# Loading a low-rank factor from SyncE's queue, behind x's first half, instead of from ScalarE's

## What is computed

```python
def qlora_linear(x, q, scale, bias, la, lb):       # la: 32 x 256, lb: 256 x 32
    w = (q / 7.5 - 1) * repeat(scale, 16)          # q: integer codes 0 to 15
    return x @ w.T + bias + (x @ la.T) @ lb.T
# branch 1: xn + linear attention(xn) (16 heads of 16, elu + 1), then a layer norm with gamma and beta
# branch 2: three blocks h = qlora(gelu(layernorm(qlora(h)))) + h, with h = xn at the start
out = x + branch1(xn) + branch2(xn)
```

## Time and profile before

| | us |
|---|---|
| median of 3 runs | 616.52 |
| lowest and highest | 616.03, 617.02 |
| the profiled execution, its whole time | 616.88 |
| its span | 615.2 |
| TensorE busy in the span | 590.7 |
| VectorE busy | 526.9 |
| ScalarE busy | 402.8 |
| GpSimd busy | 373.9 |

### The profile page before, as it was taken

How to read it: one execution, slowest core, us unless ns; L and a number is a source line. 1 busy time by engine, 2 the same in 40 slices (tenths; PEclk the granted TensorE clock), 3 DMA queues, 4 the chain that set the end, 5 groups by cost and what they waited for, 6 DMA issues and landing times.

```text
span 615.2 us, 10218 instructions
## 1 busy us (share of the span) xinstructions
PE 590.7 (96%) x3285; PEld 498.3 (81%) x3285; DVE 526.9 (86%) x1164; ACT 402.8 (65%) x619; POOL 373.9 (61%) x361
## 2 busy tenths in 40 slices
PE   6999999999999999999999999999999999999986
PEld 5778879778897889868797788978889688987865
DVE  3679899798888989889897988979898898989797
ACT  2776656848667577766768576684876667775552
POOL 5745766557644766457665575556754576746574
PEclk9999999999999999999999999999999999999999
DMA  9103000500032000500004000230004000030001
GB/s 241 62 2 136 1 2 35 170 2 0 1 125 80 0 0 18 180 6 0 0 35 170 0 0 0 87 118 0 0 0 173 32 0 0 34 102 1 0 2 69
DMA packets 11461, 29.00 MB, mean 47 GB/s; under 512 B 2593, under 2 KB 4273, under 8 KB 11441
## 3 DMA queue, kind: packets, MB, share of 16 engines
q1 hardware_dynamic: 10960, 28.35, 13.7%
q10 hardware_dynamic: 480, 0.41, 0.3%
HBM read 20.37 MB, written 8.39 MB: 47 GB/s over the span
## 4 chain that ended last, share of the span: by engine, by line
PE 70%; ACT 9%; POOL 7%; DVE 6%; issue 6%; DMA 1%; ACTq 1%; DVEq 0%; POOLq 0%
PE bank L1478 19%; PE bank L1484 9%; PE bank L1594 7%; PE bank L1605 7%; PE bank L1649 6%; PE bank L1551 4%; PE bank L1616 4%; PE bank L1570 3%; ACT fw L630 3%; POOL gl L262 2%; ACT L630 2%; PE bank L1578 2%; PE bank L1561 2%; PE bank L1538 2%; PE bank L1471 2%
## 5 line engine op out<-in xcount | busy, mean ns | idle before, releaser
L262 POOL TENSOR_TENSOR gl<-fw,gh 128x512 fp32r<-128x512 f32 x80 | 104.2, 1319 | 49.4 <-DVE gh L937 37.5
L417 POOL TENSOR_TENSOR sqs<-fw 128x512 f32<-128x512 f32 x48 | 62.8, 1309 | 73.8 <-ACT fw L620 73.7
L620 ACT ACTIVATE fw<-bank,b1c 128x512 f32<-128x512 f32 x96 | 62.3, 686 | 57.8 <-PE bank L1484 57.8
L630 ACT ACTIVATE fw<-fw,vec 128x512 f32<-128x512 f32 x96 | 74.6, 808 | 14.2 <-DVE fw L923 13.9
L923 DVE SCALAR_TENSOR_TENSOR fw<-bank,b1c,rb 128x512 f32<-128x512 f32 x96 | 67.7, 745 | 16.1 <-ACT rb L626 15.8
L267 POOL TENSOR_TENSOR hTl<-hT,hTh 128x512 fp32r<-128x512 f32 x40 | 54.1, 1368 | 39.8 <-ACT hTh L639 33.0
L392 POOL TENSOR_TENSOR rsf<-vef,neghalf 128x4 f32<-128x4 f32 x48 | 50.6, 1055 | 43.7 <-DVE vef L914 43.0
L1605 PE MATMUL bank<-K,XN 128*128 128x256 f32 x256 | 61.7, 382 | 0.0
L1649 PE MATMUL bank<-M,qT 128*128 128x256 f32 x256 | 59.4, 379 | 0.0
L392 POOL TENSOR_TENSOR rs<-ve,neghalf 128x2 f32<-128x2 f32 (+1 forms) x48 | 41.9, 874 | 22.8 <-DVE ve L1020 17.1
L1605 PEld LDWEIGHTS bank<-K,XN 128*128 128x128 f32 x256 | 46.5, 190 | 7.6 <-DVE K L982 2.0
(11 more groups left out here) (157 smaller groups left out, 1593.0 us busy)
## 6 DMA issues: line engine op xcount, KB each, us to landing
X<-in_L_attn_x_dram SPq DMA_DIRECT2D x16, 512.0 KB, 6.7
RES<-in_L_attn_x_dram SPq DMA_DIRECT2D x16, 512.0 KB, 4.3
out_dram<-RES SPq DMA_DIRECT2D x14, 512.0 KB, 2.7
XNB<-in_L_ffn_qweights_dram SPq DMA_DIRECT2D x2, 512.0 KB, 6.6
out_dram<-RES SPq DMA_DIRECT2D x4, 256.0 KB, 2.1
RES<-in_L_ffn_qweights_dram SPq DMA_DIRECT2D x1, 512.0 KB, 8.8
Y<-in_L_ffn_lora_a_dram ACTq DMA_DIRECT2D x4, 96.0 KB, 6.6
Wp<-in_L_attn_Wq_dram SPq DMA_DIRECT2D x1, 256.0 KB, 7.6
```

The costliest lines, as they stand in the source:

```text
L262: engine.tensor_tensor(gl[:, h, m, :], fw[:, h, m, :], gh[:, h, m, :].bitcast(F32), ALU.subtract).then_inc(g_low[h][m], 1)
L417: pool.tensor_tensor(sqs[:, h, :], fw[:, h, 0, :], fw[:, h, 1, :], ALU.add).then_inc(sqs_ready[h], 1)
L620: act.activation(fw[:, h, m, :], FB[h][m][:], ACT.Square, bias=b1c[:, m, j:j + 1]).then_inc(sq_ready[h], 1)
L630: act.activation(fw[:, h, m, :], fw[:, h, m, :], ACT.Gelu, bias=lnb[:, m, j:j + 1], scale=lng[:, m, j:j + 1]).then_inc(g_ready[h], 1)
```

## The change

The four transfers of A are issued by SyncE directly after x's first half and ahead of lb. They carry the same bytes to the same place and raise the same semaphore. ScalarE issues its seven short vectors as before and then goes on.

```diff
@@ -274,6 +274,12 @@
+            def load_lora():
+                for l in range(2):
+                    for c in range(NC):
+                        sp.dma_start(la[(2 * l + c) * R:(2 * l + c + 1) * R],
+                                      lora_a.rearrange("(j two) r d -> two r j d", two=2)[l]).then_inc(w_la, 16)
+
@@ -319,6 +325,7 @@
             def head():
                 load_x(0, 0)
+                load_lora()
                 load_small()
                 load_codes(0)
@@ -574,12 +581,6 @@
-            def load_lora():
-                for l in range(2):
-                    for c in range(NC):
-                        act.dma_start(la[(2 * l + c) * R:(2 * l + c + 1) * R],
-                                      lora_a.rearrange("(j two) r d -> two r j d", two=2)[l]).then_inc(w_la, 16)
-
@@ -692,7 +693,6 @@
             def head():
                 load_vectors()
-                load_lora()
                 ln1_normalise(0, 0, None)
```

## The result

The changed kernel takes 619.47 us (median of 5 runs, 618.57 to 619.63) against 616.58 us for the kernel before (5 runs, 616.03 to 617.02): a ratio of 1.0038, 95% interval 1.0027 to 1.0049. It is slower, by 2.9 us between the medians. The profiled execution took 619.47 us with a span of 617.7, against 616.88 and 615.2.

A forecast was written before the change was run, and what follows sets the result against it. TensorE, busy 96% of the span, was taken as the bound. A gain of 1.95 us less 1.51 of transfer and 0.68 of pace gave +0.24 us: 616.8 us, range 615.4 to 618.3.

The forecast's parts named there:

- rival 2: lb lands at 8.35, filler behind it slow throughout, L1745 at 15.0: 1.9 us slower, 618.4 us; chance 0.18.
- Weight 0 was hidden: GpSimd scales weight 0 near 11.0 us, before TensorE's L1739 is ready for it at 12.7: no cost.
- The step from L1676 to L1745: On TensorE, from the bias vectors' transposes to the product of A: 0.95 us.
- A's way: Transfer of A's 0.393 MB ahead of lb at 260 GB/s: 1.51 us, so lb lands at 7.35 instead of 5.84.
- 7.67 for lb by its issue alone: lb's landing if issued at 3.07 instead of 1.24 with its 4.6 us way unchanged; set aside for the queue's bytes.
- the filler's pace: The 24 filler rows behind lb run partly slow after the pause: 0.68 us lost, L1676 at 12.4.
- Both times for the step: Step to TensorE's fast pace: at 10.2 us if work before the pause counts, at 12.3 if not.
- the upper bound, all slow: All 24 filler rows behind lb at the slow pace: 4.92 us, L1676 at 13.1.
- Hidden, by 0.1: VectorE's weight 0 mean, behind six masked copies, ends at 15.8, before ScalarE's L688 can begin at 15.93: no cost.
- K: Start of L1676, the bias vectors' transposes on TensorE: 10.21 us before, forecast at 12.4.
- 1.95: Most that removing TensorE's wait for A could gain in us: L1745 at 11.16 instead of 13.11.

The follow-up runs named there:

- run 2: Changed kernel with all four filler groups ahead of lb's transposes, so TensorE has no pause: 616.31 us, ratio 0.9998 to the kernel before.
- run 6: Changed kernel without the three filler groups behind lb's transposes, the first group kept: 618.36 us, ratio 1.0026 to the kernel before.
- run 1: Changed kernel with A still on SyncE but directly behind lb (x, lb, A, scales, codes 0): 618.16 us, ratio 1.0018 to the kernel before.
- run 10: Changed kernel with A moved behind codes 0 in SyncE's queue (x, lb, scales, codes 0, A): 616.24 us, ratio 0.9984 to the kernel before.
- run 8: Changed kernel with SyncE's loads reordered (A behind codes 0, several others moved) and all filler ahead of lb's transposes: 615.46 us, ratio 0.9974 to the kernel before.
- run 5: Kernel before, with all four filler groups ahead of lb's transposes and A still on ScalarE's queue: 616.89 us, ratio 1.0010.
- run 12: Changed kernel measured again without any edit, 12 runs: 618.73 us, ratio 1.0029 to the kernel before.
- run 3: Kernel before, with lb alone moved behind scales and codes 0, A staying on ScalarE's queue: 620.07 us, ratio 1.0063.
- run 7: Changed kernel with one filler group more ahead of lb's transposes, nothing taken from behind: 617.84 us, ratio 1.0021 to the kernel before.
- run 9: Changed kernel with the load order of run 8, but the filler where it was in the kernel before: 616.02 us, ratio 0.9984 to that kernel.
- run 4: Changed kernel with lb's transposes written to an idle bank of their own: 618.56 us, ratio 1.0036 to the kernel before.
- run 11: Changed kernel with A behind lb and scales, ahead of codes 0: 617.59 us, ratio 1.0007 to the kernel before.

## Why the prediction was wrong

The forecast was no change, +0.24 us; the measured 619.47 lies above the range, whose end was 618.3. What happened is rival 2, which had 0.18. In the first profile its L1745, put at 15.0, came at 14.92: lb was 2.2 us later and not 2.5, and nearly all of the filler was slow, as given. What this profile lost beyond those 1.9 us is the wait for the bank, which no part of the prediction has.

**Right.** The wait for A vanished and the wait for lb took its place. Codes 0, Wq, Wk and the codes of weights 2 and 3 stayed hidden: L1739 had no wait for GpSimd in the changed kernel, at weight 0 or at weight 2. Weight 0 was hidden by less than it seemed: it was scaled at 11.69, not near 11.0, since its codes landed at 9.7 and not at 9.1. The step from L1676 to L1745 was put at 0.95 and is 0.99. Runs 2 and 6 show that the cover of codes 0 is the filler itself: with L1676 at 10.3 or 9.0, weight 0 waits 1.5 to 2.5 us.

**Wrong, first: A's way, "I take A at the 260 GB/s of its own stretch, 1.51 us".** lb landed at 8.07 instead of 5.84, 2.2 us later and not 1.5. The row chosen had A in it, but beside other transfers in the other queue. Where mostly A moved, the rate was lower: 191 GB/s in run 1 from 5 to 7 us, and in run 10 from 7 to 9 us:

```profile
7.00:9.00 2.00, 2.00 (x11) 2.00 (x11) 0.35 (x4) 0.00 (x0) 1.30 (x3) 1.00 0.98 195
```

At that rate A's 0.393 MB take 2.0 us. The 1.8 us worked out from the Trainium skill (SBUF — State Buffer, the section on the DMA port swizzle) was nearer; the measured rates lie below the about 218 GB/s that this section has for 32 partitions. The later issue has a part in it too. The prediction had 7.67 for lb by its issue alone and set it aside for the bytes, and 8.07 is nearer to that than to 7.35. The packets show both: lb's first came 1.8 us behind its issue, where x's, with nothing ahead of it, came 1.0 behind its own, and lb's last ended at 7.25 instead of 5.33. No run separates the two parts. In all, this term was short by 0.7 us.

**Wrong, second: the filler's pace, "I take 12.4".** The 24 rows took 5.06 us, not the 4.23 that lie between 8.17 and 12.4. Both times for the step took the 4.8 us of one profile as fixed. It is not: with no pause at all the fast pace came 3.3, 5.0 and 5.7 us behind the first filler row (runs 8, 5 and 2). The first execution of the changed kernel came close to the upper bound, all slow. This term was short by 0.8 us in that profile. Run 12's profile has 3.80 us, less than the 4.23 forecast, so this term moves by over 1 us from execution to execution, and one profile can't size it. Both together put L1676 at 13.93 (12.4 forecast).

**Wrong, third: "Hidden, by 0.1".** The prediction saw that six masked copies end at K + 2.50 and asked only who waits for them on VectorE, the mean of weight 0. It missed who waits on TensorE: the copies read lb's bank, and the fourth user of that ring of three banks is xn's first transposes. They can't start before about K + 2.56, whatever A does: the changed kernel and runs 1, 3, 7, 9, 10 and 12 all have 2.55 or 2.56, with the wait for L1061 in front. In the kernel before, TensorE's order shows them at K + 3.87, behind the wait for A, when the bank was long free:

```profile
14.08 1.04 PE L1471 MATMUL bank<-ident,XN 128*128 128x128 f32 x8
```

Run 4 takes this wait away and shows 0.6 to 0.7 us in the trace. The same term also cuts the gain that was sought: even with K unchanged at 10.21, L1471 could not have started before 12.8, so the change could give at most 1.3 us there, not 1.95. Run 12 shows this term almost alone: its L1745, at 13.50, is 0.15 from the forecast, and weight 2's transposes are still 1.04 us later than before, not 0.24.

The steps add up: 0.24 forecast, 1.57 from L1745's shift (14.92 against 13.35), 0.6 from the bank, 2.4 in all, and weight 2's transposes are 2.47 later. The profiled executions differ by 2.59 us, the medians by 2.9 and, in run 12's set, by 1.8.

**Open.** Why lb lands later when A directly follows it: with nothing more ahead of it, it took 5.6 us (run 1), 5.1 with the scales between (run 11), 4.7 with scales and codes between (run 10), 4.6 in the kernel before. The packets of these traces narrow it. lb's last packet ended at 5.67, 5.37, 5.55 and 5.33 us, in that order of the runs, so its bytes were at most 0.34 us later than before; the landing came 1.2, 1.0, 0.4 and 0.5 us behind that. What came late was mostly the report that lb was complete. Why A's packets behind it hold that up is not shown. In run 3 lb took 6.6 us where bytes alone gave about 5.3, with bo directly behind it. Open too is what in an execution sets the time of the step, beside the pause.

## What to carry to other kernels

When a transfer is moved ahead in a queue, look first at what is waited for next behind it, and by whom: here 0.4 MB ahead of lb cost more than the wait for A that it removed, and the same move three places further back (run 10) was a gain. Filler that is there to bring TensorE to its full pace belongs where TensorE would otherwise rest, ahead of the wait and not behind it; behind a pause of 1.4 us or more the fast pace came at 10.84 us or later, otherwise at 9.77 or earlier. (Where another wait follows anyway, as for A in the kernel before, the filler's place brought nothing: run 5.) And where a wait is taken away, list the users of every buffer that was free only because of it.

## What the runs showed of the hardware

- Filler of the same length took 2.77 to 5.06 us. The fast pace began at 10.84 to 13.66 us where TensorE had paused for 1.4 us or more after its first rows, and at 6.73 to 9.77 us where it had paused for less than 1 us or not at all. In run 6, with the pause and without the filler behind it, it began only at 17.8 us. The Trainium skill (TensorE: Matmul & The Clock Gate, the section on why this matters for kernels) says to avoid long idle gaps; here gaps of 1.40 us (run 1) and 2.66 us, early in the program and before the first step to the fast pace, already went with slow filler. The longest pause, 3.46 us (run 3), did not go with the slowest (4.16 us).
- The same kernel's profiled executions had their step to the fast pace at 13.66 and 10.84 us, with lb's landing only 0.2 us apart. The profile's granted clock read 1.00 in the slow stretches too: the slow rows are 0.21 us apart and the fast ones 0.11, and only that shows the step.
- A transfer's landing depended on what followed it in the queue: 4.6 to 5.6 us for lb, with the same issue time. With A directly behind, lb's landing came 1.2 us after its last packet, and 0.5 in the kernel before.
- Four transfers to 32 partitions each, one behind the other, moved at 191 (run 1) and 195 GB/s (run 10). The stretch just ahead in run 10, from 5 to 7 us, with the codes of weights 0 and 1 for all 128 partitions as most of its bytes, had 351 GB/s.
